# When guest units of the maxima may enter a feed-forward pass: one at a time while VectorE keeps up, or two in a run once both bank pairs are free

## The chip, the cores and the metric

The kernel runs on one core of one Trainium2 chip. The metric is the device time of one execution in microseconds. Its time is the median of three runs: 985.68 us (984.72 to 986.29).

## The reference

A macaron block over 2048 tokens of width 256. All layers work in float32, and the feed-forward weights come as 4-bit codes with a scale for each block of 32.

```python
x = x + 0.5 * ffn(layernorm(x))          # hidden width 2048: (gelu(x Wg) * (x Wu)) Wd
qkv = layernorm(x) @ w_project.T         # 16 heads of 16, causal
att = softmax(where(causal, -1e9, q k / 4))
x = x + (att v) @ w_out.T
x = x + 0.5 * ffn(layernorm(x))
```

## The kernel before

**Tiling.** The tokens are cut into four chunks of 512 columns. A feed-forward pass (FFN) takes one chunk through all 2048 hidden units; FFN 0 to 3 are the first layer, FFN 4 to 7 the last. An attention pass takes one chunk of queries against all keys up to it: attention 0, 1, 2, 3 have 4, 8, 12, 16 steps for each of four groups of four heads. After a first stretch written out by hand, the passes run in this order: FFN 1, FFN 2, attention 0, FFN 3, attention 1, FFN 4, attention 2, FFN 5, attention 3, FFN 6, FFN 7.

**A feed-forward pass on TensorE.** There are 16 gate products and 16 up products, alternating, each of six matmuls of 512 columns over 128 rows (lines 1122 to 1124; float32 is split into two halves, three products of halves are kept). Then come four output tiles of four parts each, a part being eight matmuls (lines 1151 and 1152). Behind a gate product ScalarE computes the gelu (line 770), behind an up product VectorE multiplies the two (line 931), ScalarE and GpSimd split the result (lines 740 and 651). Behind each output tile VectorE runs two residual operations (lines 939 and 942). Gate and up products use PSUM banks 0 to 3, output tiles too.

**An attention pass.** Each step has two pairs of scores (line 1298) into banks 0 to 3, two exponentials on ScalarE (line 760), and one product with the values (line 1315) into bank 4.

**The maxima pass.** The softmax needs the maximum of each score row before the scores are computed for good. So all scores are first computed once in another orientation, and only their maxima are kept. This is cut into 320 units. A unit is two matmuls that hold 48 rows of the array each (line 1270), of 128 to 512 columns, and on the diagonal four small masking matmuls (line 1282). VectorE then reduces both banks: in one instruction (line 1062) where the two banks are the pair 4, 5 or the pair 6, 7, and in two (line 1059) else. When a group's units are done, VectorE folds and negates ("negate"), TensorE transposes them ("rows") and a DMA puts them where the scores read them.

**The guests.** Units of the maxima are put between the products of FFN passes and between the scores of attention passes. In an FFN pass they have banks 4 to 7, as two pairs used in turn; in an attention pass banks 5 to 7 in a ring. Other guests of an FFN pass are the steps that end the attention before it (`chain`: "o", "split", "project") and those that prepare the next (`project_in`: "statistics", "transpose", "qk", "v").

**The planner.** `the_order()` runs while the kernel is built. It keeps the clocks `pe`, `act`, `dve` and `pool` of a model of its own, and writes one order that all engines' programs follow. In its model a gate or up product or an output part costs TensorE 1.3; a unit of 512 columns costs TensorE 0.24, 0.1 more when the work before it was of another kind, and VectorE 1.23 (0.08 + 512/960 for each bank); the multiplication costs VectorE 0.78, the residual 1.0. `bank_end[b]` is when VectorE will have read bank `b`, and `start_of(item)` is when the banks of the next item are free and its data there. After each gate, up or output part, `fill_ffn` puts up to two guests. In attention, `fill_attention` puts a unit where a credit allows, and `pace` raises the credit by the units left over the places left, counting 36 places for each FFN pass to come.

**The order it writes now.** Of the 320 units, 168 are in FFN passes (24, 36, 33, 37, 38 in FFN 1 to 5) and 152 in attention passes (20, 40, 55, 37). The 168 stand in 126 runs: 84 of one unit and 42 of two.

Of the kernel before, what the change touches and what calls it, by code (L numbers as in the profile page):

```python
# [5 lines left out]
def macaron_block(nc, x, w_project, w_out, gate_packed, gate_scales, up_packed, up_scales,  # L6
# [41 lines left out]
    with ctx:  # L48
# [161 lines left out]
        def the_order():  # L210
# [5 lines left out]
            pe, act, dve, pool = 0.0, 0.0, 0.0, 0.0  # L216
            mode, solo, turn, ring = None, True, 0, 0
            bank_end, end = [0.0] * 8, {("transpose", 1): 0.0}
# [17 lines left out]
            def banks_of(kind):  # L236
                if solo:
                    return ((4, 5), (6, 7))[turn]
                return tuple(5 + (ring + k) % 3 for k in range(2 if kind == "max" else 1))
# [5 lines left out]
            def start_of(item):  # L245
                kind, n, u = item
                if kind in ("negate", "statistics"):
                    return 0.0
                ready = {"max": ("stacks", n // NG), "rows": ("negate", n), "o": ("copy", NG * (n // TPC) + NG - 1),
                         "split": ("o", n), "project": ("split", n), "transpose": ("normal", n)}.get(kind)  # L250
                if kind in ("qk", "v"):
                    ready = ("transpose", 2 + 2 * n)
                return max([end.get(ready, 1e9)] + [bank_end[b] for b in banks_of(kind)])

            def put(item):
                nonlocal pe, act, dve, pool, turn, ring
                kind, n, u = item
                if kind == "negate":
                    dve = end[kind, n] = max(dve, pe) + 1.1
                    order.append(item + (None,))  # L260
                    return
                if kind == "statistics":
                    dve = max(dve, pe) + 2.2
                    pool = end["normal", n] = max(pool, dve) + 4.5
                    order.append(item + (None,))
                    return
                at = banks_of(kind)
                run("rows" if kind == "max" else "full", cost_of(item), start_of(item))
                if kind in ("transpose", "qk"):
                    act = max(act, pe + LAG) + 1.02  # L270
                    dve = max(dve, act + 0.1)
                if kind == "max":
                    dve = max(dve, pe + LAG)
                    for b in at:
                        dve += (0.08 if solo else 0.155) + u[3] / 960
                        bank_end[b] = dve
                else:
                    dve = max(dve, pe + LAG) + COST[kind][1]
                for b in at:
                    if kind != "max" or solo:  # L280
                        bank_end[b] = dve
                end[kind, n] = dve
                if kind == "qk" and u:
                    end["stacks", n] = dve + 20.5
                if kind == "rows":
                    end["in", n] = dve + 3.0
                if solo:
                    turn = 1 - turn
                else:
                    ring += len(at)  # L290
                order.append(item + (at,))

            def fill_ffn():

                done = 0
                while done < 2:
                    for queue in (chain, project_in, todo):
                        if queue and start_of(queue[-1]) <= pe + 0.05 and (queue[-1][0] != "max" or dve <= pe + 2.0):
                            done += queue[-1][0] not in ("negate", "statistics", "rows")
                            put(queue.pop())  # L300
                            break
                    else:
                        return

            def ffn(cc):
# [9 lines left out]
                for n in range(NT):  # L315
                    for kind in ("gate", "up"):
                        b = n % 2 + (0 if kind == "gate" else 2)
                        ready = (gelu_end if kind == "gate" else prod_end).get((cc, n - 2), bank_end[b])
                        run("full", 1.3, max(ready, end["transpose", INPUT_JOB[cc]]))
                        order.append((kind, cc, n, None))  # L320
                        if kind == "gate":
                            act = gelu_end[cc, n] = max(act, pe + LAG, inter_end.get((cc, n - 3), 0.0)) + 0.69
                            if n:
                                act = max(act, prod_end[cc, n - 1]) + 0.62
                                pool = inter_end[cc, n - 1] = max(pool, act) + 1.15
                        else:
                            dve = prod_end[cc, n] = max(dve, pe + LAG, gelu_end[cc, n]) + 0.78
                        if n == NT - 3:
                            while chain and kind == "gate":
                                put(chain.pop())  # L330
                        fill_ffn()
                    if not asked and n >= 6 and not chain and len(project_in) < 4:
                        put(("statistics", job, None))
                        asked = True
# [8 lines left out]
                for m in range(TPC):  # L343
                    for k in range(4):
                        ready = inter_end[cc, 4 * k + 3] if m == 0 else 0.0
                        run("full", 1.3, max(ready, gelu_end[cc, 14 + m] if m < 2 else prod_end[cc, 12 + m]))
                        order.append(("down", cc, (m, k), None))
                        if k == 3:
                            dve = bank_end[m] = max(dve, pe + LAG) + 1.0
                        fill_ffn()  # L350
# [1010 lines left out]
```

## Time and profile before

| what | value |
|---|---|
| median of three runs | 985.68 us |
| the profiled execution | 984.11 us |
| its span, first to last instruction | 982.4 us |
| mean granted TensorE clock | 0.993 |
| TensorE busy | 925.5 us (94%) |
| VectorE busy | 612.3 us (62%) |
| ScalarE busy | 478.1 us (49%) |
| maxima units on TensorE (line 1270) | 640 matmuls, 109.0 us |

The share of the span says what an engine does on average; what a change is worth is read stage by stage. In rows of the trace, PE is TensorE's matmuls, PEld its weight loads, DVE is VectorE, ACT ScalarE and POOL GpSimd. A matmul's duration overlaps with the next one's, so the distance from start to start is what it costs.

### The profile page before, as it was taken

What the parts mean: (1) busy time and instruction counts of PE and PEld (TensorE: products, weight loads), DVE (VectorE), ACT (ScalarE), POOL (GpSimd) and SP (SyncE); (2) the same over time, 40 slices, a digit from 0 to 9 for tenths busy, and PEclk for the clock granted to TensorE, in tenths of its full rate; (3) what the DMA queues carried; (4) which work ended last, traced back from release to release, by engine and by line L of the source; (5) the groups of instructions that cost most, each with busy time, mean ns of one, the idle gap of its engine ahead of it and who ended that gap; (6) DMA issues with size and microseconds to landing.
All of it is one profiled execution on the core that took longest, in us unless ns stands there. A gap on an engine that the chain in (4) does not pass through costs nothing.

```text
span 982.4 us, 16789 instructions
## 1 busy us (share of the span) xinstructions
PE 925.5 (94%) x6726; PEld 408.9 (42%) x6726; DVE 612.3 (62%) x996; ACT 478.1 (49%) x652; POOL 230.8 (23%) x261
## 2 busy tenths in 40 slices
PE   5989989999989999888999999999999998999998
PEld 3546545544534544233544322244432222445444
DVE  7993436666777678677688767768875550342221
ACT  2552432144075330877331489853229999642240
POOL 4771671225003330000441000014200000052240
PEclk9999999999999999999999999999999999999999
DMA  7000070042000150000070000000000000000000
GB/s 264 1 1 1 1 107 2 1 82 28 1 2 2 53 56 2 1 2 2 1 108 1 22 2 1 2 1 1 1 22 2 1 2 2 2 1 1 22 1 21
DMA packets 19771, 20.26 MB, mean 21 GB/s; under 512 B 3056, under 2 KB 18416, under 8 KB 19696
## 3 DMA queue, kind: packets, MB, share of 16 engines
q1 hardware_dynamic: 18048, 17.76, 9.2%
q10 hardware_dynamic: 1648, 1.44, 0.4%
q8 instruction: 54, 0.88, 0.4%
q14 instruction: 21, 0.17, 0.1%
HBM read 12.78 MB, written 6.29 MB: 19 GB/s over the span
## 4 chain that ended last, share of the span: by engine, by line
PE 80%; ACT 6%; DVE 6%; issue 5%; DMA 1%; SPq 0%; POOL 0%; ACTq 0%; DVEq 0%; POOLq 0%
PE ps L1122 12%; PE ps L1151 12%; PE ps L1124 11%; PE ps L1123 11%; PE ps L1315 9%; PE ps L1270 7%; PE ps L1152 6%; ACT inter L760 6%; PE ps L1298 4%; DVE sg L1062 2%; DVE sg L1059 1%; PE ps L1282 1%; PE ps L1109 1%; PE ps L1241 1%; DMA qreg<-qk_split 1%
## 5 line engine op out<-in xcount | busy, mean ns | idle before, releaser
L760 ACT ACTIVATE inter<-ps 128x1024 f32<-128x1024 f32 (+3 forms) x320 | 266.0, 898 | 33.3 <-PE ps L1282 18.6
L651 POOL TENSOR_TENSOR inter<-wreg,inter 128x512 f16<-128x512 f32 x112 | 129.2, 1157 | 643.9 <-ACT inter L740 643.7
L1062 DVE TENSOR_REDUCE sg<-ps 128x2 f32<-128x1024 f32 (+3 forms) x217 | 220.1, 1036 | 50.6 <-PE ps L1282 25.7
L770 ACT ACTIVATE wreg<-ps,gelu_in 128x512 f32<-128x512 f32 x112 | 77.0, 688 | 260.5 <-PE ps L1124 260.4
L1151 PE MATMUL ps<-wd,inter 128*128 128x512 f16 x512 | 170.9, 381 | 0.0
L1059 DVE TENSOR_REDUCE sg<-ps 128x1 f32<-128x512 f32 (+3 forms) x206 | 120.7, 631 | 63.2 <-PE ps L1270 42.5
L931 DVE SCALAR_TENSOR_TENSOR wreg<-ps,kappa,wreg 128x512 f32<-128x512 f32 x128 | 95.4, 746 | 94.7 <-PE ps L1124 89.0
L1315 PE MATMUL ps<-inter,v 128*17 128x512 f32 (+3 forms) x1280 | 149.6, 540 | 0.7
L1152 PE MATMUL ps<-wd,inter 128*128 128x256 f16 x512 | 139.6, 273 | 0.0
L1270 PE MATMUL ps<-kreg,qreg 48*128 48x512 f16 (+3 forms) x640 | 109.0, 354 | 19.1 <-DVE sg L1062 11.6
L1298 PE MATMUL ps<-qreg,kreg 50*128 50x512 f16 (+3 forms) x640 | 110.0, 354 | 16.0 <-ACT inter L760 10.4
L1122 PE MATMUL ps<-xT,wg 128*128 128x512 f16 x256 | 99.4, 388 | 1.4 <-DVE xT L896 1.4
L1124 PE MATMUL ps<-xT,wg 128*128 128x512 f16 x256 | 98.8, 386 | 0.0
L1123 PE MATMUL ps<-xT,wg 128*128 128x512 f16 x256 | 98.8, 386 | 0.0
L1122 PE MATMUL ps<-xT,wu 128*128 128x512 f16 x256 | 97.4, 381 | 0.0
L1123 PE MATMUL ps<-xT,wu 128*128 128x512 f16 x256 | 97.1, 379 | 0.0
L1124 PE MATMUL ps<-xT,wu 128*128 128x512 f16 x256 | 97.1, 379 | 0.0
L740 ACT ACTIVATE inter<-wreg 128x512 f16<-128x512 f32 x128 | 79.5, 622 | 12.9 <-DVE wreg L931 12.7
L1298 PEld LDWEIGHTS ps<-qreg,kreg 50*128 50x128 f16 x640 | 31.5, 93 | 114.9 <-ACT inter L760 102.1
L1270 PEld LDWEIGHTS ps<-kreg,qreg 48*128 48x128 f16 x640 | 29.8, 93 | 118.4 <-DVE sg L1062 42.9
L1151 PEld LDWEIGHTS ps<-wd,inter 128*128 128x128 f16 x512 | 50.0, 98 | 63.6 <-issue 9.7
L760 ACT ACT_TABLE_LOAD x4 | 5.1, 1283 | 103.9 <-PE ps L1152 103.9
(130 smaller groups left out, 893.3 us busy)
## 6 DMA issues: line engine op xcount, KB each, us to landing
qk_split<-oT SPq DMA_DIRECT2D x4, 1024.0 KB, 4.4
kreg<-qk_split SPq DMA_DIRECT2D x24, 128.0 KB, 4.8
qreg<-qk_split SPq DMA_DIRECT2D x24, 128.0 KB, 8.4
out_x<-xres SPq DMA_DIRECT2D x4, 512.0 KB, 2.9
xres<-in_L_attn_x SPq DMA_DIRECT2D x3, 512.0 KB, 9.3
kreg<-in_L_ffn_gate_W_packed SPq DMA_DIRECT2D x4, 256.0 KB, 6.5
kreg<-in_L_ffn_up_W_packed ACTq DMA_DIRECT2D x4, 256.0 KB, 7.9
kreg<-in_L_ffn_down_W_packed SPq DMA_DIRECT2D x1, 1024.0 KB, 10.9
```

The source lines that it names most:

```text
L651: pool.tensor_tensor(inter[:, 1, u, :], prod_ring[:, u % 3, :], inter[:, 0, u, :], ALU.subtract).then_inc(s_inter, 1)
L760: act.activation(p_ring[:, pair % 8, :, 0:w], ps[:, 512 * b:512 * b + 1024].rearrange("p (a q) -> p a q", a=2)[:, :, 0:w], ACT.Exp, scale= ...
L1059: dve.tensor_reduce(m_part[:, r, part, col + 8 * a:col + 8 * a + 1], bank(at[a], width), AX.X, ALU.max).then_inc(s_slot_read, 1)
L1062: dve.tensor_reduce(m_part[:, r, part, col:col + 9:8], both[:, :, 0:width], AX.X, ALU.max).then_inc(s_slot_read, 1)
L1122: pe.matmul(dst, w[:, 0, kt, cols], xT[buf][:, 0, kt, :], start=(kt == 0), stop=False)
L1123: pe.matmul(dst, w[:, 0, kt, cols], xT[buf][:, 1, kt, :], start=False, stop=False)
L1124: last = pe.matmul(dst, w[:, 1, kt, cols], xT[buf][:, 0, kt, :], start=False, stop=(kt == KT - 1))
L1151: pe.matmul(down_bank(m), inter[:, 0, n, tok], wd[:, n, :], start=(n == 0), stop=False)
L1152: last = pe.matmul(down_bank(m)[:, 0:D], inter[:, 1, n, tok], wd[:, n, 0:D], start=False, stop=(n == NT - 1))
L1270: last = pe.matmul(bank(at[a], w), qreg[c % 2][rows, pair, q0:q0 + P], kreg[rows, pair, k0:k0 + w], start=True, stop=part < c)
L1298: last = pe.matmul(dst[a], kreg[rows, pair, P * j:P * j + P], qreg[c % 2][rows, pair, q0:CT], start=True, stop=j < TPC * c)
L1315: last = pe.matmul(bank(4, CT - q0, q0)[32 * h:32 * h + HD + 1, :], v1[:, j, GH * g + h, :], p_ring[:, b % 8, h % 2, 0:CT - q0], start=(j ...
```

## The change

One condition in `fill_ffn`. Before, a unit of the maxima could be put when its own pair of banks was free and VectorE's clock stood at most 2.0 ahead of TensorE's. Now it is put when something was already put in this fill (`done`), or when all four guest banks 4 to 7 are free. The condition on VectorE's clock is gone. All else (costs, pace, queues, the limit of two) is as it was; units that find no place in an FFN pass are put later, in attention.

```diff
@@ -295,7 +295,8 @@
                 done = 0
                 while done < 2:
                     for queue in (chain, project_in, todo):
-                        if queue and start_of(queue[-1]) <= pe + 0.05 and (queue[-1][0] != "max" or dve <= pe + 2.0):
+                        if queue and start_of(queue[-1]) <= pe + 0.05 and \
+                                (queue[-1][0] != "max" or done or max(bank_end[4:8]) <= pe + 0.05):
                             done += queue[-1][0] not in ("negate", "statistics", "rows")
                             put(queue.pop())
                             break
```

## Rows read from the trace of the kernel before

**Rows 1.** Windows: length, busy PE, PEld, DVE, ACT, POOL; granted clock, DMA share, GB/s.

```profile
185.30:271.00 85.70, 85.70 (x549) 41.06 (x546) 58.91 (x91) 23.78 (x37) 25.61 (x30) 1.00 0.19 32
271.00:302.40 31.40, 25.57 (x412) 11.27 (x405) 24.22 (x41) 23.24 (x36) 0.00 (x0) 1.00 0.01 2
...
391.70:459.90 68.20, 57.47 (x652) 18.30 (x648) 47.24 (x78) 54.73 (x68) 0.00 (x0) 0.97 0.01 2
459.90:551.70 91.80, 91.70 (x554) 44.50 (x549) 72.75 (x109) 25.57 (x38) 25.71 (x30) 1.00 0.19 30
551.70:647.00 95.30, 86.70 (x874) 23.79 (x870) 65.79 (x103) 84.18 (x100) 0.00 (x0) 0.98 0.02 7
...
730.50:847.20 116.70, 108.39 (x1014) 27.15 (x1014) 47.05 (x73) 113.10 (x132) 0.00 (x0) 1.00 0.02 6
```

**Rows 2.** Timeline of TensorE in FFN 1: two products with no guest between.

```profile
100.56 0.38 PE L1122 MATMUL ps<-xT,wg 128*128 128x512 f16 x1
...
101.85 0.38 PE L1122 MATMUL ps<-xT,wu 128*128 128x512 f16 x1
```

**Rows 3.** Timeline of TensorE in FFN 2: one unit between two products.

```profile
235.68 0.39 PE L1122 MATMUL ps<-xT,wg 128*128 128x512 f16 x1
...
236.76 0.38 PE L1124 MATMUL ps<-xT,wg 128*128 128x512 f16 x1
237.07 0.39 PE L1270 MATMUL ps<-kreg,qreg 48*128 48x512 f16 x2
237.40 0.39 PE L1122 MATMUL ps<-xT,wu 128*128 128x512 f16 x1
```

**Rows 4.** Timeline of TensorE in FFN 2: two units between two products.

```profile
228.78 0.38 PE L1122 MATMUL ps<-xT,wg 128*128 128x512 f16 x1
...
230.17 0.61 PE L1270 MATMUL ps<-kreg,qreg 48*128 48x512 f16 x4
230.71 0.39 PE L1122 MATMUL ps<-xT,wu 128*128 128x512 f16 x1
```

**Rows 5.** Timeline in FFN 2's output parts: weight loads and matmuls from a unit on.

```profile
248.61 0.11 PEld L1270 LDWEIGHTS ps<-kreg,qreg 48*128 48x128 f16 x4 [0.32 <-DVE sg L1062]
248.62 0.60 PE L1270 MATMUL ps<-kreg,qreg 48*128 48x512 f16 x4
...
249.15 0.10 PEld L1151 LDWEIGHTS ps<-wd,inter 128*128 128x128 f16 x1 [0.42 <-issue]
249.17 0.10 PEld L1152 LDWEIGHTS ps<-wd,inter 128*128 128x128 f16 x1
249.38 0.27 PE L1152 MATMUL ps<-wd,inter 128*128 128x256 f16 x1
```

**Rows 6.** Timeline of VectorE in FFN 2: the pair's reductions, then a multiplication.

```profile
230.60 2.36 DVE L1062 TENSOR_REDUCE sg<-ps 128x2 f32<-128x1024 f32 x2 [0.82 <-PE ps L1270]
232.87 0.74 DVE L931 SCALAR_TENSOR_TENSOR wreg<-ps,kappa,wreg 128x512 f32<-128x512 f32 x1
233.53 0.96 DVE L1062 TENSOR_REDUCE sg<-ps 128x2 f32<-128x256 f32 x2
```

**Rows 7.** Timeline of VectorE in FFN 2's output parts: a residual, then a unit.

```profile
256.63 0.48 DVE L939 SCALAR_TENSOR_TENSOR half_sum<-ps,s_down,xres 128x256 f32<-128x256 f32 x1 [1.28 <-PE ps L1152]
...
257.55 0.20 DVE L1052 COPY sd<-ps 32x128 f16<-32x128 f16 x1
```

**Rows 8.** Timeline in attention 1: weight load of a unit waiting for VectorE.

```profile
406.02 0.10 PEld L1270 LDWEIGHTS ps<-kreg,qreg 48*128 48x128 f16 x2 [0.85 <-DVE sg L1062]
```

**Rows 9.** Waits in attention 3 (waiter, awaited: us in all, times, longest).

```profile
PEld ps L1298 <- ACT inter L760: 68.7, 104, 0.9
```

**Rows 10.** Timeline in attention 3: a unit, then the next pair of scores.

```profile
781.30 0.38 PE L1270 MATMUL ps<-kreg,qreg 48*128 48x512 f16 x2
781.60 0.10 PEld L1298 LDWEIGHTS ps<-qreg,kreg 50*128 50x128 f16 x2 [0.41 <-ACT inter L760]
```

**Rows 11.** Waits of TensorE over the whole span.

```profile
PE ps L1298 <- DVE xres L942: 3.2, 4, 1.5
```

## The prediction, made before the run

> **What bounds the kernel now.** I read the windows by stage first, since the change touches the FFN passes directly and the attention passes by what is left over for them. In FFN 2 TensorE is busy for all of the 85.70 us, in FFN 4 for 91.70 of 91.80; VectorE is at 58.91 and 72.75 [rows 1]. FFN 3 and 5 look the same. So in these passes every nanosecond that TensorE issues is in the span, and VectorE has room on average. Attention 3 is another regime: ScalarE is busy for 113.10 of 116.70 us [rows 1], and the list of waits there is led by scores that wait for an exponential, 68.7 us in 104 waits [rows 9]. Attention 0, 1 and 2 lie between: TensorE 25.57 of 31.40, 57.47 of 68.20 and 86.70 of 95.30 us, ScalarE 23.24, 54.73 and 84.18 [rows 1]; no engine is full, and the order decides.
>
> Then I read single products in the timeline, by start to start. A gate product with nothing behind it takes 101.85 - 100.56 = 1.29 us [rows 2]. With one unit of 512 columns behind it, 237.40 - 235.68 = 1.72 us [rows 3], with two, 230.71 - 228.78 = 1.93 us [rows 4]. So one unit alone costs 0.43 us and the pair 0.64. The second costs 0.21, and what is left of the first, 0.43 - 0.21 = 0.22 us, is paid once for a run, whatever its length. It sits at both edges: the last matmul of the product to the unit is 237.07 - 236.76 = 0.31 us, where six matmuls in 1.29 us are 0.215 apart; and the unit to the next product is 0.33 us [rows 3]. The weight loads show the same: inside an output part the load of line 1152 starts at 249.17, its matmul at 249.38, so it is done ahead; at the unit (248.61 and 248.62) load and matmul start together, and at the unit's far side the load is at 249.15 after a gap put down to issue [rows 5].
>
> **The change part by part.**
>
> *Runs that disappear.* The planner's order of before has 168 units in 126 runs in the FFN passes, 84 of them with one unit. Under the new condition a run headed by a unit always gets its second: all four banks are free when the first goes in, so the other pair is free when the second is asked. Singles remain only where a chain or input item took the first place in a fill, or the products end; I allow 5. How many units still fit is set by the planner's own clocks, so I take them for the count, and for no time. In them a cycle of two products and a run of two is 2.6 + 0.2 + 0.49 = 3.29 on TensorE, and VectorE needs 2 x 1.23 + 0.78 = 3.23. After the run starts, VectorE is done with both banks 0.34 + 0.35 + 2.45 = 3.15 later, the second product ends at 3.29: the run goes in after every second product, with 0.14 to spare. Two units for each gate and up pair is what the order of before reaches with singles of 512 columns, too. With output parts, two runs in four parts need 6.57 of TensorE and 5.9 of VectorE, so 16 units in 16 parts, where the old order has 16 to 21, because a part alone could already have a unit. Small units (128 and 256 columns) lose most: the old condition let three or four of them in beside a pair of products. Pass by pass I get 24, 32, 28 to 30, 30 to 32, 33 to 35, in all about 157 instead of 168, and 157/2 plus singles, 83 runs. Saved: 43 runs x 0.22 = 9.4 us. Bounds: 75 to 95 runs, 51 to 31 fewer, 11.2 to 6.8 us.
>
> *Units that leave.* 11 units fewer at 0.21 us: 2.3 us less in the FFN passes (bounds 4 to 23 units, 0.8 to 4.8 us).
>
> *Where they go.* Each costs the same 0.21 to 0.23 us of TensorE in an attention pass, without an edge: scores are themselves products of less than the full rows, and the unit at 781.30 is followed by scores at 781.60 which waited for ScalarE anyway [rows 10]. In attention 3 this wait is there in nearly every step [rows 9], so a unit is free there; what hides it is the exponential, and with the cover gone it costs 0.23. In attention 0 to 2 the lower bound is nothing, the upper 0.85 us, the wait of a unit's weight load for VectorE in attention 1 [rows 8], plus 0.23, so 1.08. Attention 1 stands still on TensorE for 68.20 - 57.47 = 10.7 us with 40 units [rows 1], 0.27 for each if all of it is theirs, and attention 2 for 8.6 with 55. I take 0.35 on these, nearer to this average than to the single row, and put 7 of the 11 there and 4 into attention 3: 7 x 0.35 = 2.4 us back.
>
> *VectorE's condition removed.* Does TensorE now meet VectorE in the FFN passes? By rows, the two reductions and the multiplication take 2.27 + 0.66 = 2.93 us from start to start (230.60, 232.87, 233.53) [rows 6], against 2.58 + 0.64 = 3.22 on TensorE. For four output parts it is 4 x 1.14 + 0.92 (residual, 256.63 to 257.55 [rows 7]) = 5.5 against 6.4. So VectorE keeps up with 0.3 us in each cycle, better than the model thinks: 0 us, up to 2 if single waits come out. The multiplication can stand behind two reductions, up to 2.3 us late; behind it wait ScalarE's split, GpSimd's and the third gate product later, which has more than 3 us; only the last one before the output parts is near, and those need it only in their fourth part, some 4 us on. At a pass's end the last residual can stand behind two reductions, and the first scores wait for it: that wait is 3.2 us in four places now [rows 11]; I add 0.3, bounds -1 and +3.
>
> *Sum.* -9.4 - 2.3 + 2.4 + 0.3 = -9.0 us. The profiled execution took 984.11 us (span 982.4), so 975.1 for one like it. The median shown is 985.68, 1.57 above; on that footing the forecast is 976.7, which is what I give.
>
> *A rule against it.* The Trainium skill, page "TensorE: Matmul & The Clock Gate", section "Step-by-step: what each phase is for", says that weight loads are pulled ahead of matmuls in flight when their row groups don't conflict or when they go to the background buffer. By that a run's edge could cost nothing, and the first term of the sum would be 0 instead of 9.4 us. The trace has the pull-ahead inside a part and not at the unit [rows 5], so the sum goes by the rows.
>
> **The rivals.**
>
> *Half of it comes back.* More units leave than I think, 20 and over, because negate, statistics and the residual push VectorE's clock past the one free moment and a run slips by a whole product. Then 90 runs are left (7.9 saved), 20 units leave (4.2), and 16 of them at 0.6 in attention 0 to 2 come back as 9.6, with the 0.3: -2.2 us, 983.5; with fewer leaving, down to -5, 980.7. For it: the margin of 0.14 in the planner's cycle. Against it: the slip costs only one product of 16.
>
> *Slower: units stall attention.* The same units at the price of rows 8, 1.08 us each, in attention 0 to 2, whose groups have deadlines. Its gain side is 9.4 + 0.21 for each that leaves; it decides once 9.4 < n x (1.08 - 0.21), that is from 11 units all in attention 0 to 2. With 16 there and 20 leaving, 83 runs: -9.4 - 4.2 + 17.3 + 0.3 = +4.0, 989.7. For it: the 0.85 us waits are common in attention 1. Against it: TensorE's whole standstill there is 0.27 for each unit, and attention 3 takes its part free.
>
> *The edge is not a cost.* The 0.22 us could be an offset that another wait would fill, or a load done ahead when runs stand elsewhere. Then only units move: -2.3 + 2.7 = +0.4, 986.1. Against it: TensorE is occupied all through FFN 2 [rows 1], and the product with two units is only 0.21 us longer than that with one [rows 3, 4]. The Trainium skill's rule above would give this case.
>
> **How the numbers follow.** Forecast (-5 to -12.5 us) 0.74; half comes back 0.13; the edge is no cost, or gain and return cancel, 0.06; slower 0.07. What a measurement of this kernel can tell is about 0.2%, 2 us. Faster by more is the first two, 0.87; within it 0.06; slower 0.07. The forecast's own range is 973 to 981; for 8 in 10 with the bounds of runs, units and stage ends I give 972 to 983.5, which takes in the second case and leaves out the last two.
>
> **What would show it.** Right: runs of one unit nearly gone from the FFN passes and 80 to 88 runs left; FFN 2 to 5 shorter by about 10 to 12 us together, at the same 1.93 us for a product with two units; no waits for VectorE in them; attention 0 to 2 longer by 2 to 3 us together, attention 3 unchanged with more units. Wrong: fewer than 150 units in the FFN passes, or attention 1 or 2 more than 3 us longer (first two rivals); a product with two units above 2.0 us or new waits of line 1270 in FFN passes (VectorE as the bound); FFN passes shorter only by the units that left (third rival).

## The result and the profile after

The changed kernel takes 993.25 us (median of four runs, 992.13 to 993.58) against 985.98 of before: ratio 1.0073, interval 1.0056 to 1.0091, so slower by 7.3 us. 976.7 was forecast, and 972 to 983.5 as the range. The profiled execution has a span of 991.3 us, 8.9 more than before.

The change adds one line, so line 1270 of before is 1271 here, 1298 is 1299, and so on. Windows by stage of the changed kernel (length, then busy PE, PEld, DVE, ACT, POOL, granted clock) are FFN 2, attention 0, FFN 4, attention 2, FFN 5 and attention 3:

```profile
181.60:265.00 83.40, 83.40 (x545) 41.19 (x544) 55.48 (x88) 23.95 (x37) 25.70 (x30) 1.00 0.19 33
265.00:296.40 31.40, 25.39 (x403) 11.05 (x399) 23.39 (x41) 23.20 (x36) 0.00 (x0) 1.00 0.01 2
...
448.80:534.80 86.00, 86.00 (x517) 43.76 (x509) 61.52 (x99) 25.45 (x38) 25.79 (x30) 1.00 0.19 32
534.80:638.60 103.80, 88.61 (x908) 26.04 (x907) 76.62 (x122) 86.03 (x100) 0.00 (x0) 0.98 0.02 7
638.60:716.90 78.30, 78.30 (x465) 38.34 (x463) 57.83 (x90) 22.61 (x36) 22.09 (x23) 1.00 0.00 1
716.90:856.10 139.20, 118.54 (x1085) 29.31 (x1082) 73.65 (x113) 115.72 (x132) 0.00 (x0) 0.94 0.02 5
```

Against [rows 1], FFN 2 is 2.3 us shorter and FFN 4 5.8. Over FFN 1 to 5, from one pass's first matmul to the next one's, it is -3.9, -2.3, -3.9, -5.8 and -5.1: 21.1 us gained before rounding, over twice what the forecast had. It is lost again behind it: attention 0 and 1 stand at +0.1 and -1.3, attention 2 at +8.5 (95.3 to 103.8), attention 3 at +22.5 (116.7 to 139.2).

The order that the changed planner writes explains the shift. The FFN passes hold 134 units instead of 168 (20, 34, 24, 26, 30), in 71 runs instead of 126; attention holds 20, 42, 64, 60 instead of 20, 40, 55, 37. By groups, attention 3 has 20, 20, 20, 0 units where it had 13, 14, 10, 0. Windows of its four groups, first before and then after:

```profile
730.50:760.10 29.60, 27.24 (x262) 6.96 (x261) 17.40 (x29) 28.88 (x33) 0.00 (x0) 1.00 0.06 19
760.10:789.00 28.90, 27.77 (x264) 6.88 (x260) 15.96 (x23) 28.09 (x33) 0.00 (x0) 1.00 0.00 1
789.00:817.90 28.90, 27.52 (x265) 7.05 (x261) 13.68 (x22) 28.06 (x33) 0.00 (x0) 1.00 0.01 2
817.90:847.00 29.10, 25.66 (x236) 6.23 (x232) 0.00 (x0) 28.07 (x33) 0.00 (x0) 1.00 0.00 1
```

```profile
716.90:753.70 36.80, 31.54 (x284) 7.71 (x282) 23.91 (x36) 29.61 (x33) 0.00 (x0) 0.91 0.05 15
753.70:787.10 33.40, 28.98 (x289) 7.49 (x287) 24.05 (x39) 28.84 (x33) 0.00 (x0) 1.00 0.01 2
787.10:825.20 38.10, 29.53 (x293) 7.88 (x289) 25.70 (x40) 29.06 (x33) 0.00 (x0) 0.96 0.01 2
825.20:856.10 30.90, 28.49 (x233) 6.24 (x234) 0.00 (x0) 28.21 (x33) 0.00 (x0) 0.88 0.00 1
```

Before, a group takes about 29 us with 14 units, with 10 and with none: they are free. After, the second group, which shows the effect alone (clock 1.00, ScalarE's work unchanged), takes 33.4 with 20: six units more, 4.5 us. The last group, without a unit, is 1.8 us longer at a granted clock of 0.88.

The waits of that second group, longest first in total, show who sets the pace, before and then after:

```profile
PEld ps L1298 <- ACT inter L760: 17.2, 26, 0.9
```

```profile
PEld ps L1271 <- DVE sg L1063: 6.9, 6, 1.6
PEld ps L1271 <- DVE sg L1060: 5.8, 8, 1.1
PEld ps L1299 <- ACT inter L761: 4.2, 7, 0.8
ACT inter L761 <- PE ps L1299: 3.3, 9, 0.7
```

Scores that waited for ScalarE have become units that wait for VectorE to read their banks, 12.7 us, and ScalarE in its turn waits for scores, 3.3 us where it was 0.5. At the end of the third group something else is late. The timeline of TensorE's last unit there, and what follows:

```profile
819.58 0.39 PE L1271 MATMUL ps<-kreg,qreg 48*128 48x512 f16 x2
...
821.90 0.17 DVE L1007 SCALAR_TENSOR_TENSOR m_split<-su,m_split 128x16 f16<-128x16 f32 x1
...
822.22 0.22 PE L1258 MATMUL ps<-ident,m_split 128*32 128x128 f16 x1 [2.19 <-DVE m_split L1007]
...
822.71 1.25 SPq L528 DMA_DIRECT2D qreg<-sd  x2
825.15 0.21 PEld L1299 LDWEIGHTS ps<-qreg,kreg 50*128 50x128 f16 x4 [2.87 <-DMA qreg<-sd]
...
825.80 1.94 ACT L761 ACTIVATE inter<-ps 128x1024 f32<-128x1024 f32 x2 [6.20 <-PE ps L1299]
```

The last unit of the last group's maxima stands right before that group's first scores. Reduction, fold, transposition and DMA follow one another with nothing beside them, and ScalarE has nothing for 6.20 us. In the order of before 11 pairs of scores stood between.

What a unit costs in an FFN pass is as the prediction had it. In FFN 5, an up product and two units after it, TensorE, and VectorE's rows for the stretch before:

```profile
679.59 0.38 PE L1123 MATMUL ps<-xT,wu 128*128 128x512 f16 x1
...
680.98 0.60 PE L1271 MATMUL ps<-kreg,qreg 48*128 48x512 f16 x4
681.52 0.39 PE L1123 MATMUL ps<-xT,wg 128*128 128x512 f16 x1
```

```profile
675.36 0.75 DVE L932 SCALAR_TENSOR_TENSOR wreg<-ps,kappa,wreg 128x512 f32<-128x512 f32 x1 [0.71 <-PE ps L1125]
677.95 0.75 DVE L932 SCALAR_TENSOR_TENSOR wreg<-ps,kappa,wreg 128x512 f32<-128x512 f32 x1 [1.84 <-PE ps L1125]
```

681.52 - 679.59 = 1.93 us, as in [rows 4]. VectorE stands idle for 0.71 and 1.84 us between its tasks: there was time for more units, and the planner did not place them.

### The profile page after: what moved, and what is told of

The parts are those of the page before. It is cut to its first block, busy times and chain, and to the rows that moved or that the text cites. A ratio compares the mean times of both kernels' runs of the same rounds, so it can differ in the third digit from the quotient of the medians.

```text
span 991.3 us, 16799 instructions
## 1 busy us (share of the span) xinstructions
PE 918.2 (93%) x6726; PEld 412.0 (42%) x6726; DVE 612.4 (62%) x1021; ACT 483.0 (49%) x652; POOL 231.6 (23%) x261
## 4 chain that ended last, share of the span: by engine, by line
PE 82%; DVE 8%; ACT 4%; issue 3%; DMA 1%; POOL 1%; SPq 1%; ACTq 0%; DVEq 0%; POOLq 0%
PE ps L1123 12%; PE ps L1152 12%; PE ps L1125 11%; PE ps L1124 11%; PE ps L1316 11%; PE ps L1271 8%; PE ps L1153 6%; PE ps L1299 4%; DVE sg L1063 4%; DVE sg L1060 3%; ACT inter L761 3%; PE ps L1110 1%; PE ps L1283 1%; PE ps L1242 1%; DMA qreg<-qk_split 1%
## 5 line engine op out<-in xcount | busy, mean ns | idle before, releaser
L761 ACT ACTIVATE inter<-ps 128x1024 f32<-128x1024 f32 (+3 forms) x320 | 270.7, 897 | 58.0 <-PE ps L1299 32.7
L1063 DVE TENSOR_REDUCE sg<-ps 128x2 f32<-128x1024 f32 (+3 forms) x192 | 192.4, 1030 | 51.2 <-PE ps L1283 25.7
L1060 DVE TENSOR_REDUCE sg<-ps 128x1 f32<-128x512 f32 (+3 forms) x256 | 148.3, 627 | 60.5 <-PE ps L1271 40.7
L1316 PE MATMUL ps<-inter,v 128*17 128x512 f32 (+3 forms) x1280 | 153.2, 552 | 0.5
L1271 PE MATMUL ps<-kreg,qreg 48*128 48x512 f16 (+3 forms) x640 | 106.1, 354 | 34.4 <-DVE sg L1063 15.9
L1124 PE MATMUL ps<-xT,wu 128*128 128x512 f16 x256 | 97.2, 380 | 0.0
L1152 PEld LDWEIGHTS ps<-wd,inter 128*128 128x128 f16 x512 | 50.1, 98 | 62.0 <-issue 5.3
L1153 PEld LDWEIGHTS ps<-wd,inter 128*128 128x128 f16 x512 | 50.1, 98 | 5.5
```

Source lines behind the costliest of these rows:

```text
L761: act.activation(p_ring[:, pair % 8, :, 0:w], ps[:, 512 * b:512 * b + 1024].rearrange("p (a q) -> p a q", a=2)[:, :, 0:w], ACT.Exp, scale= ...
L1060: dve.tensor_reduce(m_part[:, r, part, col + 8 * a:col + 8 * a + 1], bank(at[a], width), AX.X, ALU.max).then_inc(s_slot_read, 1)
L1063: dve.tensor_reduce(m_part[:, r, part, col:col + 9:8], both[:, :, 0:width], AX.X, ALU.max).then_inc(s_slot_read, 1)
L1124: pe.matmul(dst, w[:, 0, kt, cols], xT[buf][:, 1, kt, :], start=False, stop=False)
L1152: pe.matmul(down_bank(m), inter[:, 0, n, tok], wd[:, n, :], start=(n == 0), stop=False)
L1153: last = pe.matmul(down_bank(m)[:, 0:D], inter[:, 1, n, tok], wd[:, n, 0:D], start=False, stop=(n == NT - 1))
```

## The experiments

Each kernel ran beside the kernel before on the same chip. "Group" is one of the four groups of an attention pass; all counts of units are those of the order that the planner wrote. Four to twelve runs each; medians and ratios as measured. The kernel before had medians of 984.4, 983.8 and 983.7 us in the three sessions, and 985.98 beside the change; where two kernels of different sessions are compared, the difference of each to its own before says more than that of the medians.

**Crowding alone: FFN 5 capped, everything up to there as before.**

```diff
-  if queue and start_of(queue[-1]) <= pe + 0.05 and (queue[-1][0] != "max" or dve <= pe + 2.0):
+  if queue and start_of(queue[-1]) <= pe + 0.05 and \
+          (queue[-1][0] != "max" or dve <= pe + 2.0 and (now_in != 5 or put_in < 15)):
```

> The kernel before with one thing added: FFN 5 may take only 15 units of the maxima (38 before). The planner then gives attention 3 20, 20, 20, 0 units in its four groups, as the change did, where before had 13, 14, 10, 0; all passes up to attention 2 are as before; 113 runs instead of 126. Theory A (the loss is the price of crowded groups in attention 3): FFN 5 gets shorter by 13 x 0.22 + 23 x 0.21 = 7.7 us, attention 3 longer by about 20 us, in all +10 to +15 us against before. Theory B (attention 3 takes units for nothing, and the loss came from waits that the new condition made): -7 us.

995.6 us, ratio 1.0116 (1.0098 to 1.0134), inside the expected +10 to +15. The order holds 110 runs, not the 113 expected: 16 fewer in FFN 5, so 16 x 0.22 + 23 x 0.21 = 8.4 us. FFN 5 went from 83.4 to 74.4 us, of which 0.8 is a wait of its transposes that is gone; attention 3 went from 116.7 to 136.8 (+20.1), each pass up to attention 2 is within 1.5. Here the old condition is in force everywhere, and the loss in attention 3 is the same as with the change. Its groups:

```profile
720.90:756.20 35.30, 30.18 (x273) 7.59 (x271) 20.94 (x33) 28.90 (x31) 0.00 (x0) 0.95 0.05 16
756.20:789.60 33.40, 28.97 (x297) 7.51 (x289) 24.06 (x39) 28.84 (x33) 0.00 (x0) 1.00 0.01 1
789.60:827.60 38.00, 30.33 (x305) 8.22 (x299) 26.62 (x41) 29.51 (x35) 0.00 (x0) 1.00 0.01 2
827.60:857.90 30.30, 27.16 (x220) 5.92 (x221) 0.00 (x0) 27.62 (x32) 0.00 (x0) 0.89 0.00 1
```

Theory A holds: the number of units decides, not how they got there.

**The same with a cap of 28** (`put_in < 28`).

> As the cap at 15, with the cap at 28: attention 3 gets 15, 16, 16, 0 units, ten more than before, 119 runs. FFN 5 gets shorter by 7 x 0.22 + 10 x 0.21 = 3.6 us. Theory A with a price only above some 14 units in a group: five units above at about 0.8 us, so attention 3 +4, in all 0 to +1 us. Theory A with an even price of about 1 us for each unit: +6 us. Theory B: -3.6 us.

992.6 us, ratio 1.0084 (1.0061 to 1.0108): both forms of theory A were off, the even price by less. FFN 5 gave the 3.6 us. In attention 3 (+11.0) the groups took 31.2, 30.6, 35.2 and 30.7 us for 15, 16, 16 and 0 units. So two units above 14 cost 1.7 us in the second group, about the price of before; the rest, some 8 us, is in the third and fourth group, where the last unit stands only 2 pairs of scores before the deadline and ScalarE again waited (5.0 us). A deadline is missed at 47 units already; the third group has 16 units as well, so not all of the 8 us is the deadline's.

**The deadline: the pace aims 8 pairs earlier, in the changed kernel and in the one capped at 28.**

```diff
-  pairs = 2 * (first_step[n] - place_now[0]) - place_now[1] - 1
+  pairs = 2 * (first_step[n] - place_now[0]) - place_now[1] - 1 - 8
```

> The kernel with the change, and the pace in attention aims each group's last unit 8 pairs of scores earlier. FFN passes as with the change (133 units), attention 20, 42, 65, 60, group 15's last unit now stands 10 pairs of scores before that group's first score (0 with the change, 11 before). Theory A (a part of the loss is one missed deadline: group 15's maxima come so late that the scores wait): the 6.2 us gap of ScalarE before group 15 goes, and the half clock behind it, -6 to -9 us against the change, about 985.5. Theory B (the loss is only the crowding, and crowding earlier costs the same): 993, no gain.

991.0 us, ratio 1.0069 (1.0044 to 1.0094). Windows of the groups:

```profile
719.10:755.90 36.80, 31.41 (x260) 7.86 (x258) 23.21 (x35) 28.40 (x29) 0.00 (x0) 0.91 0.05 15
755.90:790.60 34.70, 29.16 (x297) 8.08 (x291) 26.21 (x42) 29.17 (x33) 0.00 (x0) 1.00 0.01 1
790.60:823.00 32.40, 28.60 (x285) 7.72 (x281) 24.03 (x38) 29.00 (x33) 0.00 (x0) 1.00 0.01 2
823.00:852.20 29.20, 25.77 (x238) 6.20 (x236) 0.00 (x0) 28.14 (x34) 0.00 (x0) 1.00 0.01 1
```

The wait is gone, and third and fourth group together are 7.4 us shorter, as theory A said; three units fewer in the third group (17 for 20) are part of that. Little of it reached the end. The median is 2.3 us below that of the change, but against the before beside each, +7.2 stands against +7.3. In the profiles attention 3 is 6.0 us shorter and attention 2, which has one unit more, 2.2 longer; FFN 1 and the stretch ahead of it, whose orders are the same, took 2.3 more in this execution. The forecast 985.5 for the whole was wrong in part because I had counted the wait and not where its units go (22 in the second group: 34.7 us).

> The kernel before with FFN 5 capped at 28 units, as the earlier run with this cap, and the pace aiming 8 pairs of scores earlier: attention 3 gets 16, 17, 12, 0, attention 2 57 instead of 55, and group 15's last unit stands 9 pairs before its first score instead of 2. Theory A: about -7 us against the run with the cap alone (992.6), so 985.5, even with before, since FFN 5 gives 3.6 and the crowding of groups 12 and 13 takes 3 to 4. Theory B: stays at 992.

987.5 us, ratio 1.0042 (1.0028 to 1.0056): 5.1 us less than with the cap alone by medians, 4.4 by the differences to before, of the 7 expected. Attention 3 went from 127.7 to 122.5 us, its groups 33.3, 30.6, 29.3, 29.2.

**What makes a crowded group slow: shorter reads of the banks.** In the kernel capped at 15:

```diff
   i, hp, _, width, part = unit
+  width = min(width, P) if c == NCH - 1 else width
```

> The kernel with FFN 5 capped at 15 units (attention 3 gets 20, 20, 20, 0), and VectorE reads only the first 128 columns of each bank of the last chunk's units; the maxima of that chunk are therefore taken over a part of the columns only. TensorE's work and the order are the same. A read of one bank falls from 0.69 to 0.28 us. Theory A (a crowded group is slow because a unit waits until VectorE has read one of the three guest banks): groups 12 to 14 fall from 35.2, 33.4, 38.0 us to 29 to 31 each and attention 3 from 136.8 to about 120, attention 2 (53 of whose 55 units are of the last chunk) from 95 to 90 to 93. Theory B (the units' own TensorE time, 20 x 0.23, and their place ahead of the scores are the price): groups stay at 33 and more.

987.7 us, ratio 1.0049 (1.0033 to 1.0065), 7.9 less than the same order with full reads by medians, 7.1 by the differences to before. The second group fell from 33.4 to 30.9, inside the expected 29 to 31, attention 2 from 95.4 to 92.9. The first and the third stayed slow, 34.3 and 35.2, and attention 3 took 131.6 us where about 120 was expected: the missed deadline behind the third group is there as with full reads (ScalarE waits 5.3 us), and attention 3 had 6.8 and 10.2 us at the lower clock, where the run with full reads had 3.4 and 6.8. So VectorE's reading of the three guest banks is the larger part of the crowding price in the one undisturbed group, 2.5 of 4.5 us; 2.0 remain with the units' own TensorE time or what else stands between, which these runs don't divide.

**One part of the change alone: VectorE's condition out, nothing put in.**

```diff
-  if queue and start_of(queue[-1]) <= pe + 0.05 and (queue[-1][0] != "max" or dve <= pe + 2.0):
+  if queue and start_of(queue[-1]) <= pe + 0.05:
```

> One part of the change alone: the condition on VectorE's clock is taken out and nothing is put in its place. The planner places 175 units in 124 runs in FFN passes, attention 18, 40, 54, 33. Theory A: 7 units more at 0.21 = +1.5, 2 runs fewer = -0.4, attention about -1: 0 to +1 us against before. Theory B (that condition kept VectorE's backlog small): +3 us or more, with waits for VectorE in FFN passes.

988.6 us, ratio 1.0041 (1.0027 to 1.0055): theory B. The order holds 175 units in 124 runs, and TensorE waits for VectorE in FFN passes, where the list of before has one wait of 0.8:

```profile
PE ps L1241 <- DVE sg L1062: 3.3, 3, 1.6
```

Line 1241 is the transposes behind the last up product. They need a pair of guest banks, and when two units went in just before, they wait until VectorE has read them. The old condition kept that rare; I had priced its removal at nothing. In this run's profile FFN 1 to 5 are 3.9 us longer together, 1.0 as priced for units and runs and 2.5 for these waits. The attention passes are 2.4 us longer although they have 7 units fewer, which this run doesn't explain.

**Pairs without the loss of units: a looser test.** The change, with `+ 0.8` in both tests of a unit:

```diff
-  if queue and start_of(queue[-1]) <= pe + 0.05 and \
-          (queue[-1][0] != "max" or done or max(bank_end[4:8]) <= pe + 0.05):
+  if queue and start_of(queue[-1]) <= pe + (0.8 if queue[-1][0] == "max" else 0.05) and \
+          (queue[-1][0] != "max" or done or max(bank_end[4:8]) <= pe + 0.8):
```

> The change, with both tests of a unit of the maxima (own banks, all four banks) made against TensorE's clock + 0.8 instead of + 0.05. The planner then places 170 units in the FFN passes (168 before, 134 with the change) in 93 runs (126 before), and attention gets 20, 40, 54, 36 as before. Theory A: 33 runs x 0.22 = 7.3 us saved, 2 units more at 0.21: about -7 us against before, near 979; waits of TensorE for VectorE in the FFN passes below 2 us. Theory B (pairs make VectorE late and TensorE waits): no faster than before, waits of line 1271 in the FFN passes of 5 us and more.

985.1 us, ratio 1.001 (1.000 to 1.0019): none of the 7 us. The FFN passes are 2.6 us shorter together, not 6.9. 3.6 us, where before has 0.8, are in three waits of the transposes at the ends of FFN 2, 4 and 5; theory B had the waits, but at the units' own line, where no matmul waits for VectorE in these passes. The attention passes, with one unit fewer in each of the last two, are 3.0 us longer together, which stays open. The timeline of the wait in FFN 5:

```profile
700.89 0.60 PE L1271 MATMUL ps<-kreg,qreg 48*128 48x512 f16 x4
...
701.05 0.75 DVE L932 SCALAR_TENSOR_TENSOR wreg<-ps,kappa,wreg 128x512 f32<-128x512 f32 x1 [0.22 <-PE ps L1125]
701.72 2.35 DVE L1063 TENSOR_REDUCE sg<-ps 128x2 f32<-128x1024 f32 x2
...
702.99 1.23 PE L1242 MATMUL ps<-ident,wreg 128*128 128x128 f32 x8 [1.50 <-DVE sg L1063]
```

The next two kernels forbid a unit in that fill (`fill_ffn(kind == "gate" or n < NT - 1)`, with units skipped when it is false) and loosen the test to 0.9 and 1.0.

> The change with the two tests made against TensorE's clock + 0.9, and no unit allowed in the fill behind the last up product of a pass, in front of the transposes. 174 units in 94 runs in FFN passes (168 in 126 before), attention 18, 40, 54, 34, margin of group 15 17 pairs of scores. Theory A (edges are worth 0.22 us each, and what the earlier run at 0.8 lost again is the transposes' wait for VectorE, 4.1 us in three passes): -32 x 0.22 + 6 x 0.21 = -5.8 us in FFN passes, attention within 1 us: 978 to 980. Theory B (edges don't show in the time): 984 to 985, as the run at 0.8.

982.1 us, ratio 0.9988 (0.9970 to 1.0006): not clear of before, by 1.7 us. The FFN passes gave 1.4 us instead of 5.8. Matmuls of units now wait for VectorE's read in FFN 2, 4 and 5, 1.5 us in all with single waits up to 0.5, where before has none: a pair went in before both banks were read. The other 2.9 us were not traced.

> As the run before it, at TensorE's clock + 1.0: 185 units in 98 runs in FFN passes, attention 18, 39, 50, 28, margin of group 15 27 pairs. Theory A: -28 x 0.22 + 17 x 0.21 = -2.6 us in FFN passes; attention 2 with 5 units fewer and attention 3 with 9 fewer gain little, since groups of 14 there already run at ScalarE's pace: -1 to -2; in all 980 to 981, so no better than at 0.9. Rival (every unit in attention costs near 1 us, as the cap at 28 might suggest): 17 units x 1.0 - 2.6: below 970.

988.1 us, ratio 1.0043 (1.0021 to 1.0065). The FFN passes are 9.4 us longer instead of 2.6 shorter. The same waits come to 6.2 us here, so eleven more units bought some 5 us more of them; again the rest was not traced. The rival is out: attention 3 with 28 units takes 117.3 us, with 37 it took 116.7.

**The change's own test with VectorE's costs as the trace has them.**

```diff
-  dve += (0.08 if solo else 0.155) + u[3] / 960
+  dve += (0.04 if solo else 0.155) + u[3] / 960
-  dve = prod_end[cc, n] = max(dve, pe + LAG, gelu_end[cc, n]) + 0.78
+  dve = prod_end[cc, n] = max(dve, pe + LAG, gelu_end[cc, n]) + 0.67
-  dve = bank_end[m] = max(dve, pe + LAG) + 1.0
+  dve = bank_end[m] = max(dve, pe + LAG) + 0.91
```

with `LAG = 0.25` and the pace 6 pairs earlier.

> The change's own condition at + 0.05, with the planner's VectorE costs set to what the trace shows (a bank's read 0.04 + width/960, the multiplication 0.67, the residual 0.91, the lag 0.25), and the pace aiming 6 pairs earlier. 152 units in 79 runs in FFN passes, attention 20, 41, 61, 46, margin of group 15 8 pairs. Theory A: -47 x 0.22 - 16 x 0.21 = -13.7 us in FFN passes, no wait for VectorE there; attention 2 with 61 and attention 3 with 46 come back as +5 to +6 each: 981 to 983. Theory B (the loss of the change was the wrong VectorE costs alone): the full -13 us, 971.

993.2 us, ratio 1.0108 (1.0085 to 1.0131): both theories missed, B by more. 152 units instead of 134 are not enough; attention 2 with 61 took 103.8 us and attention 3 with 46 took 124.3, +8.5 and +7.6 where I had +5 to +6 each. The FFN passes gave 8.3 of 13.7, since the transposes behind a pair wait in four of them, 5.7 us where before has 0.8. And a deadline was missed again: the last group's last unit stands 8 pairs of scores ahead, but its "rows" step only one, and the scores wait 1.9 us for the DMA behind it. The wrong costs are a part of the lost places, not the whole.

**The same with `+ 0.5` and no unit in front of the transposes.**

> As the run before it, with both tests at + 0.5 and no unit in front of the transposes: 162 units in 87 runs, attention 20, 41, 57, 40, margin 8 pairs. Theory A: -39 x 0.22 - 6 x 0.21 = -9.8 us in FFN passes, +2 for waits for VectorE, attention +2 to +3: about 979, the fastest so far. Rival: the waits of two units entering half a microsecond early eat it, 983 and more.

983.8 us, ratio 1.0005 (0.9980 to 1.0030), in twelve runs from 977.4 to 989.7. The FFN passes gave 8.8 us, where 9.8 less 2 for waits was expected, so the edges are there to be had. Attention 3 gave back 4.4 us of it for three units more, and a part of that is a deadline. The last unit of group 15 again stands 8 pairs ahead and its "rows" step one; the first scores of the group:

```profile
810.14 0.23 PE L1258 MATMUL ps<-ident,m_split 128*32 128x128 f16 x1
...
813.10 0.61 PE L1299 MATMUL ps<-qreg,kreg 50*128 50x512 f16 x4 [1.94 <-DMA qreg<-sd]
813.53 1.94 ACT L761 ACTIVATE inter<-ps 128x1024 f32<-128x1024 f32 x2 [2.51 <-PE ps L1299]
```

With the "rows" step 5 or 7 pairs ahead, as in the two kernels with the pace 8 earlier and in before, this wait is not in the lists: the margin that counts is that of "rows", not that of the last unit. The profiled execution took 981.55 us; why the median lies 2.2 above it is the last section's subject.

## Why the prediction was wrong

- **The price of an edge and of a unit in an FFN pass: right.** In FFN 2 to 5, 49 runs fewer at 0.22 are 10.8 us and 30 units fewer at 0.21 are 6.3, together 17.1. Measured are 17.2, of which 0.8 is a wait of the transposes in FFN 5 that is gone. No matmul waits for VectorE in these four passes. FFN 1 gained 3.9 us for 6 runs and 4 units; there a DMA wait shrank from 2.8 to 1.0, a stretch of 3.4 us at the lower clock is gone and a wait of the transposes of 1.4 is new, so it tests the price less well. The third rival, the free edge, is out, and with it the reading of the Trainium skill's page "TensorE: Matmul & The Clock Gate" that I had set against rows 5.
- **How many units fit: the first failing step.** "The run goes in after every second product, with 0.14 to spare" took VectorE as free when a run starts. Behind an up product the planner's VectorE clock is already 1.13 ahead, by the multiplication just queued; then both banks are free 0.30 after the second product's end, not 0.14 before it, and the run waits for the third. 134 units instead of 157, outside the bounds that I had given (145 to 164): 34 left instead of 11. The margin of 0.14 was named as what speaks for the first rival, and dismissed with "the slip costs only one product of 16"; in the order, none of the eight pairs of 512-column units behind an up product has the next run two products later, and three of the four behind a gate product have. But the larger part of the miss is in the output parts. There I had 16 units in 16 parts, 80 in five passes; the order has 63, where before has 89. The products hold 71, before 79, and my total left 77 for them. "Two runs in four parts" holds once the runs are going, but the planner's VectorE clock is still 2.4 ahead of TensorE's behind the first output part of FFN 5, since the transposes' result is on it; in FFN 2 to 5 the first run stands behind the third part, and "negate" and "rows" take further places. With the trace's VectorE costs the products held 82 units and the output parts 70, so the output parts are where the places stayed lost. (5 singles and 76 pairs for 157 units make 81 runs, too, not 83; that is 0.4 us.)
- **Attention 3 as free: the second failing step, and the dearer one.** "In attention 3 this wait is there in nearly every step, so a unit is free there" is true up to some 14 units in a group of 16 steps and false above. It is a price read from a lightly filled pass. I sent 4 units there and 23 went. At full clock six units above 14 cost 4.5 us, 0.75 each; the cap at 15 reproduces the whole +20 us without the change. Over all kernels with full reads, attention 3 took 116.4 to 118.0 us with 28 to 37 units, 121.1 with 40, 122.5 and 124.3 with 45 and 46, 127.7 with 47, and 133.2 to 139.2 with 60, deadlines and clock included.
- **Attention 2**: nine units more at 8.5 us, 0.94 each, where I had taken 0.35 and kept 1.08 as the upper bound. The kernel with the trace's costs had only six more and took the same 103.8; 57 units took 97.2. The wait of 0.85 us in [rows 8], which I set aside as a single row, was the better guide for units at the margin; the average over all units of a pass is not.
- **Deadlines: not in the sum at all.** The pace spreads the units until the first scores of their group and counts nothing for what lies behind the last of them. With few units nothing stands there; with 60 ScalarE stood for 6.2 us before the last group. Taking that out, with three units of the third group, gave 7.4 us in two groups.
- **VectorE's condition: mis-sized.** "0 us, up to 2" stood for it. In the change itself one such wait is new in an FFN pass, 1.4 us at the transposes of FFN 1; alone its removal costs 4.2 us, in part as seven more units and as waits of the transposes.
- **The rival on the slower side** had the mechanism (units that stall attention, with deadlines), the wrong place (attention 0 to 2 alone) and 0.07. Its own point of decision, 11 units at the full price, was passed by far.

## What to carry to other kernels

An edge that is paid once for a run is worth pairing over, but the rule that makes the pairs also sets how many guests find a place; count the places by running through the planner's state from a cycle that is already loaded, not from an idle one. A slot that costs nothing at today's filling has a price from some filling on: before sending more there, find which resource refills it (here three banks and the engine that reads them) and how far the last step that a deadline needs stands from it. A price for work moved to a place is the price of the next unit there, not the average of those that are there already.

## What was not expected of the hardware

TensorE's granted clock fell to its lower level (1.2 of 2.4 GHz) for stretches of 3.4, 6.8 or 10.2 us, and the change had more of them: 27.3 us before the kernel's end, in five stretches of which four lie in attention passes, against 13.6 us in four, two of them in attention passes. Windows of the changed kernel around two of them:

```profile
716.90:720.10 3.20, 1.35 (x10) 0.32 (x6) 2.92 (x4) 3.19 (x4) 0.00 (x0) 1.00 0.48 162
720.10:727.00 6.90, 6.54 (x34) 1.00 (x32) 2.57 (x4) 3.67 (x4) 0.00 (x0) 0.51 0.00 1
813.00:819.00 6.00, 5.56 (x86) 2.14 (x86) 3.97 (x6) 4.52 (x8) 0.00 (x0) 1.00 0.01 3
819.00:822.50 3.50, 1.24 (x17) 0.39 (x15) 3.00 (x8) 0.60 (x2) 0.00 (x0) 1.00 0.00 0
822.50:832.80 10.30, 7.20 (x36) 1.01 (x36) 0.18 (x1) 6.20 (x7) 0.00 (x0) 0.50 0.00 1
```

Both times TensorE had been busy for less than half of the stretch before (1.35 of 3.20 us, 1.24 of 3.50), once at the start of the pass, once at the missed deadline. That alone doesn't decide it. The kernel before starts attention 3 with the same standstill and keeps the full clock behind it:

```profile
730.50:733.70 3.20, 1.36 (x9) 0.30 (x8) 1.72 (x4) 3.05 (x3) 0.00 (x0) 1.00 0.16 53
733.70:737.10 3.40, 3.17 (x26) 0.61 (x28) 2.47 (x4) 3.40 (x5) 0.00 (x0) 1.00 0.32 104
```

How much it weighs can be estimated from run to run, with the same program. Before: three runs of one session at a mean clock of 0.996 took 979.9 to 980.5 us, six at 0.991 took 984.1 to 986.0, which is about 1 us for 0.001 of the mean clock, or half a microsecond for each microsecond at the lower level. The last experiment: 977.4, 978.0 and 981.6 at 0.994, 988.3 to 989.7 at 0.980, which is 0.7 us for 0.001. At 0.994, where before takes 982.3 to 984.3 in the same session, all three runs of the last experiment are faster, by 0.7 us and more; it loses this in the runs in which the clock falls more often. The changed kernel had 0.988 in three runs (992.1 to 993.6 us) and 0.985 in one (993.0), so it shows no slope of its own; before had 0.991 to 0.994 mostly. By the slopes above, 0.003 to 0.006 less would be some 2 to 6 of its 7.3 us. This is a reckoning over runs and not an experiment; the stretches in attention 3 are already inside its +22.5 us and no further loss. What tips the clock in one run and not in the next was not tried, and stays open.
